# A decoder layer on one core: context clipping on GpSimd, two tiles projected chunk by chunk, quantised roots transposed by DMA

## The chip, the core and the metric

The kernel runs on one core of a Trainium2 chip. TensorE (PE) multiplies into PSUM, VectorE (DVE), ScalarE (ACT) and GpSimd (POOL) work on what it needs and leaves, and DMAs are issued from three queues: SP's, ScalarE's and GpSimd's. Every engine and every queue carries its instructions out in the order in which they are written, and waits only on semaphores. The metric is the device time of one execution in microseconds.

## What is computed

```python
# attention among the heads of one token (x: 2 x 512 x 1024; 32 heads of 32, 8 groups)
q, k, v = x @ Wq + bq, repeat(x @ Wk + bk), repeat(x @ Wv + bv)
o = softmax(q k^T / sqrt(32)) v
x = layernorm(x + o)
# quantised product with the context (2 x 1024 x 1024)
fq(y, s, z) = (clip(round(y / s + z), 0, 255) - z) * s
x = layernorm(x + matmul(fq(x), fq(ctx)))
# feed-forward: shared squared-relu part, and a routed low-rank part
h = relu(x @ up) ** 2
x = layernorm(x + layernorm(h @ down + ((x @ fc1) @ expert * sum(top2(x @ gate))) @ fc2) ...)
```

## The kernel before, in words

The program has two blocks with a barrier between them: attention_and_cross (lines 57 to 1253) and feed_forward (from line 1283). The 1024 tokens are 8 tiles of 128. Each matrix that needs more than bf16 is split in a high and a low part, and three products replace one (split_products, line 51).

**Start.** SP loads x tile 0, then the attention weights in 8 chunks of 128 rows (load_w, 0.75 MB each), then x tile 1. Each chunk passes VectorE (prepare, L886, and prepare_lo, L893), ScalarE (split_w, L603 and L604) and GpSimd (keys_values_lo, L1132). project (L341) takes 6 matmuls for each chunk, 48 for a tile. All tiles are projected into the same two PSUM banks, so tile t waits for qkv_out(t - 1).

**One tile of attention.** transpose_x (L325), xT_hi_out (ScalarE, L584) and xT_lo_out (VectorE, L968), project, qkv_out (VectorE, L964). regroup (L201) brings q, k and v from tokens on the partitions to heads, in 8 small DMAs on SP. keys_diagonal makes k_bd on GpSimd (L1178) and ScalarE (L557), values_transpose and values_diagonal make v_bd (GpSimd, L1149). Then scores (L354), softmax_max, softmax_exp and softmax_transpose, values (L371), collect, and ungroup (L206), 8 small DMAs on SP back to tokens.

**One tile of the quantised product.** residual, first_stats, inverse_deviation_x1 (GpSimd), normalise_x1, quantise_a (ScalarE, relu), magic (VectorE, clip and rounding by a large constant), quantise_b (ScalarE, into the one buffer q1). transpose_q1 (L381) turns q1 on TensorE with 8 bf16 matmuls into a PSUM bank, q1T_out (ScalarE, L564) copies it to q1T, cross (L399) multiplies, cross_out (ScalarE) evacuates, and the second layer norm follows with row_term, add_column_term and inverse_deviation_x2 on GpSimd. x2 goes to DRAM (store_x2) and comes back by load_xk.

**The context.** 16 tiles are loaded from ScalarE's queue, pass ctx_a (ScalarE, relu), ctx_magic (VectorE, L956: minimum with 255, plus the constant) and ctx_b (ScalarE, to bf16). column_sums(0) and cross(0) need the first 8 of them, column_sums(1) all 16.

**Order.** Nothing is scheduled at run time: the order of each engine is the list of calls at the end of its function (TensorE L462 to L544, ScalarE L662 to L814, VectorE L980 to L1125, GpSimd L1187 to L1253, SP L247 to L314). In the feed-forward block first_products takes the first columns, and product(2, 0) needs u_lo of column block 2, which VectorE makes in split_u (L1813) after route(0) (L1825 to L1839).

## Time and profile before

| | |
|---|---|
| median of 3 runs | 636.34 us (636.12 to 637.76) |
| the profiled execution | 638.93 us |
| its span | 637.1 us |
| TensorE busy | 595.8 us, 94% of the span |
| VectorE, ScalarE, GpSimd busy | 378.5, 299.5, 123.0 us |
| mean granted TensorE clock | 0.985 of full speed |
| attention_and_cross on TensorE | 0 to about 210 us |

The profile is of one execution. Busy time of TensorE is modelled from pipelined matmuls, so the useful reading is where it stands idle and what ended that: the chain of work that ended last runs through TensorE for 64% of the span. Of the last 2.6 us between the profiled execution and the median nothing is known from the trace.

### The profile page before, as it was taken

The page shows a single profiled execution, that of the slowest core. Times are in us where ns is not written, and L with a number is a line of the kernel's source. Part 1 is how long each engine was busy: PE and PEld are TensorE (multiplying, and loading weights), DVE is VectorE, ACT ScalarE, POOL GpSimd, SP SyncE. Part 2 cuts the span into 40 slices and gives each one's busy share as a digit, 9 for nine tenths or more (in the row PEclk, how much of TensorE's full clock was granted, in tenths as well). Part 3 has the DMA queues.
Part 4 walks back from the last instruction along what each step waited for, and adds up shares of the span by engine and source line. Part 5 has one row for each costly group of instructions (what it writes and reads, how often), then busy time and mean ns, then how long its engine had stood idle before and what let it go on. Part 6 is the DMA issues. An engine that isn't in the chain of part 4 may idle for free.

```text
span 637.1 us, 9378 instructions
## 1 busy us (share of the span) xinstructions
PE 595.8 (94%) x3718; PEld 479.8 (75%) x3728; DVE 378.5 (59%) x515; ACT 299.5 (47%) x384; POOL 123.0 (19%) x162
## 2 busy tenths in 40 slices
PE   2789999998999879999999999999999999999993
PEld 1578877675776658788888888888888888888882
DVE  4746989789854353155235331138974565749976
ACT  4545778896684433333434333004354433323824
POOL 2711245645432022232220000000000000011000
PEclk9889999998999989999999999999999999999998
DMA  9756675583663657789888683402333336079913
GB/s 332 278 141 199 177 226 128 179 280 108 194 200 133 232 192 260 272 296 343 318 315 291 219 306 118 137 1 79 120 99 100 100 99 224 8 265 323 285 57 128
DMA packets 82252, 123.61 MB, mean 194 GB/s; under 512 B 23840, under 2 KB 50720, under 8 KB 82208
## 3 DMA queue, kind: packets, MB, share of 16 engines
q1 hardware_dynamic: 74592, 94.95, 44.5%
q0 software_dynamic: 5168, 19.40, 9.4%
q10 hardware_dynamic: 2448, 8.65, 4.1%
q8 instruction: 30, 0.49, 0.3%
q14 instruction: 14, 0.11, 0.1%
HBM read 83.13 MB, written 35.65 MB: 186 GB/s over the span
## 4 chain that ended last, share of the span: by engine, by line
PE 64%; DVE 2%; ACT 0%; issue 0%; DVEq 0%; ACTq 0%
PE psum L1552 33%; PE psum L1611 30%; PE psum L1519 0%; PE psum L1527 0%; PE psum L1528 0%; PE psum L1545 0%; DVE r_tok L1834 0%; DVE ffn_lo L1959 0%; DVE ffn_lo L1948 0%; ACT hx L1714 0%; DVE u_lo L1813 0%; ACT ffn_lo L1724 0%; DVE hx L1839 0%; PE psum L1536 0%; DVE stat_n L1940 0%
## 5 line engine op out<-in xcount | busy, mean ns | idle before, releaser
L1813 DVE TENSOR_TENSOR u_lo<-u_raw,u_hi 128x1024 fp32r<-128x1024 f32 x18 | 25.5, 1420 | 85.2 <-ACT u_hi L1650 85.2
L1552 PE MATMUL psum<-x1T_hi,u_hi 128*128 128x512 f32 x160 | 62.9, 393 | 0.7 <-DVE x1T_lo L1809 0.7
L1552 PE MATMUL psum<-x1T_hi,u_lo 128*128 128x512 f32 x160 | 62.3, 389 | 0.0
L1552 PE MATMUL psum<-x1T_lo,u_hi 128*128 128x512 f32 x160 | 62.3, 389 | 0.0
L1611 PE MATMUL psum<-x2T_lo,x2T_hi 128*128 128x512 f32 x264 | 62.1, 389 | 0.0
L1552 PE MATMUL psum<-x2T_hi,u_hi 128*128 128x512 f32 x144 | 57.0, 396 | 4.6 <-DVE u_lo L1813 4.6
L1611 PEld LDWEIGHTS psum<-x2T_lo,x2T_hi 128*128 128x128 f32 x264 | 49.6, 188 | 10.3
L1552 PE MATMUL psum<-x2T_lo,u_hi 128*128 128x512 f32 x144 | 56.8, 394 | 0.0
L1552 PE MATMUL psum<-x2T_hi,u_lo 128*128 128x512 f32 x144 | 56.6, 393 | 0.0
L341 PE MATMUL psum<-w_hi,xT_hi 128*128 128x512 f32 (+1 forms) x128 | 36.1, 364 | 15.7 <-POOL w_lo L1132 8.2
L1611 PE MATMUL psum<-x1T_hi,x2T_hi 128*128 128x512 f32 x216 | 50.4, 389 | 0.0
L1611 PE MATMUL psum<-x1T_hi,x2T_lo 128*128 128x512 f32 x216 | 50.4, 389 | 0.0
L2090 POOL DMA_DIRECT2D x1T_hi<-r_scratch x4 | 2.8, 711 | 245.3 <-PE psum L1611 245.3
L1611 PEld LDWEIGHTS psum<-x1T_hi,x2T_lo 128*128 128x128 f32 x216 | 40.6, 188 | 8.4
L1611 PEld LDWEIGHTS psum<-x1T_hi,x2T_hi 128*128 128x128 f32 x216 | 40.6, 188 | 8.4
L341 PEld LDWEIGHTS psum<-w_hi,xT_hi 128*128 128x128 f32 x128 | 21.0, 200 | 20.7 <-issue 8.8
L1552 PEld LDWEIGHTS psum<-x1T_hi,u_hi 128*128 128x128 f32 x160 | 30.1, 188 | 7.4 <-issue 0.9
L1552 PEld LDWEIGHTS psum<-x2T_hi,u_hi 128*128 128x128 f32 x144 | 27.4, 190 | 10.5 <-issue 4.7
L1552 PEld LDWEIGHTS psum<-x1T_hi,u_lo 128*128 128x128 f32 x160 | 30.0, 188 | 6.3
L1552 PEld LDWEIGHTS psum<-x1T_lo,u_hi 128*128 128x128 f32 x160 | 30.0, 188 | 5.9
L341 PE MATMUL psum<-w_hi,xT_lo 128*128 128x512 f32 (+1 forms) x128 | 34.5, 352 | 0.0
L341 PE MATMUL psum<-w_lo,xT_hi 128*128 128x512 f32 (+1 forms) x128 | 34.2, 350 | 0.0
(258 smaller groups left out, 1218.3 us busy)
## 6 DMA issues: line engine op xcount, KB each, us to landing
d_raw<-in_L_ffn_down_w_dram SPq DMA_DIRECT2D x20, 512.0 KB, 7.7
t_scratch<-d_raw SPq DMA_DIRECT2D x20, 512.0 KB, 6.8
d_raw<-t_scratch SPq DMA_DIRECT2D x20, 512.0 KB, 3.8
c_sb<-in_ctx_dram ACTq DMA_DIRECT2D x16, 512.0 KB, 3.9
u_raw<-in_L_ffn_up_w_dram SPq DMA_DIRECT2D x16, 512.0 KB, 5.3
r_scratch<-f1b SPq DMA_DIRECT2D x10, 512.0 KB, 5.7
r_scratch<-f2b SPq DMA_DIRECT2D x10, 512.0 KB, 5.9
x_sb<-in_x_dram SPq DMA_DIRECT2D x8, 512.0 KB, 4.9
```

The lines of the kernel that those rows point to most:

```text
L341: mm = pe.matmul(qkv_ps[:, c0:c1], s, v, start=(k == 0 and i == 0), stop=(k == KT - 1 and i == 2))
L1552: mm = pe.matmul(acc_b[:, product_index(m, b) % 4], s, v, start=(k == 0 and i == 0), stop=(k == KT - 1 and i == 2))
L1611: mm = pe.matmul(acc_of(phase)[:, t], a, v, start=(k == 0 and i == 0), stop=(k == NP - 1 and i == 2))
L1813: dve.tensor_tensor(u_lo[:, m % 2], u_raw[:, m % 2], u_hi[:, m % 2].bitcast(F32), ALU.subtract).then_inc(S["u_lo_done"], 1)
L2090: pool.dma_start(ob[ob_slot(s)].rearrange("p s h c -> p s (h c)"), r_dram[k * P:(k + 2) * P, n].rearrange("(s p) h c -> p s (h c)", p=P)). ...
```

## The change

ctx_magic moves from VectorE to GpSimd. Tiles 0 and 1 are projected chunk by chunk in turns as the weights come (project_early), tile 1 into the banks of the quantised product (qkv_of), and x tile 1 is loaded after weight chunk 3. The first two context loads wait for the last weight chunk. Of the 8 DMAs of regroup and of ungroup GpSimd issues 4, on semaphores of their own. transpose_q1 is an SP DMA that transposes q1 straight into q1T; the TensorE transposes and q1T_out are gone. store_x2 of the last two tiles has a semaphore of its own. All five lists of calls in attention_and_cross are written in a new order, and in the feed-forward block split_u(2) stands ahead of route(0).

```diff
+        qkv_of = lambda t: xa_ps if t == 1 else qkv_ps
+        SP_OUT = 4
+        SP_BLOCKS = 4
# sync
-                for n in range(NG):
+                for n in range(SP_BLOCKS):
                     sp.dma_start(pg[:, t % 2, n], qkv_sb[rows16(n), t % 2]).then_inc(pg_in[t % 2], 16)
+            def transpose_q1(t):
+                sp.wait_ge(S["q1_done"], t + 1)
+                if t >= 2:
+                    sp.wait_ge(S["xa_ready"], t - 1)
+                sp.dma_start_transpose(q1T[:, t % 2], q1[:]).then_inc(q1T_in[t % 2], 16)
             for k in range(KT):
                 load_w(k)
-            load_x(1)
+                if k == 3:
+                    load_x(1)
# tensor
+            def project_early(t, k):
+                if k == 0:
+                    pe.wait_ge(S["xT_lo_done"], t + 1)
+                pe.wait_ge(S["wq_lo_done"], k + 1)
+                pe.wait_ge(S["wkv_lo_done"], k + 1)
+                mm = contract(t, k)
+                if k == KT - 1:
+                    mm.then_inc(S["qkv_ready"], 1)
             def cross(t):
-                pe.wait_ge(S["q1T_done"], t + 1)
+                pe.wait_ge(q1T_in[t % 2], 16 * (t // 2 + 1))
+                if t >= 1:
+                    pe.wait_ge(S["xa_evac"], t)
             transpose_x(0)
-            project(0, 0)
+            project_early(0, 0)
             transpose_x(1)
-            project(0, 1)
-            project(1, 0)
-            project(1, 1)
+            project_early(0, 1)
+            project_early(0, 2)
+            project_early(1, 0)
+            project_early(1, 1)
+            project_early(1, 2)
+            project_early(1, 3)
+            project_early(0, 3)
+            project_early(0, 4)
+            project_early(0, 5)
             transpose_x(2)
+            project_early(0, 6)
+            project_early(0, 7)
+            project_early(1, 4)
...
+            project_early(1, 7)
+            project(2, 0)
             scores(0)
-            project(2, 0)
+            project(2, 1)
             values(0)
-            project(2, 1)
+            scores(1)
             transpose_x(3)
-            scores(1)
             project(3, 0)
...
             project(7, 0)
-            transpose_q1(3)
+            values(5)
+            cross(3)
             scores(6)
             project(7, 1)
-            cross(3)
-            values(5)
             transpose_expert(0)
             transpose_expert(1)
             column_sums(1)
             values(6)
             transpose_expert(2)
             transpose_expert(3)
-            transpose_q1(4)
             scores(7)
+            transpose_x2(0)
             cross(4)
# scalar
-            def q1T_out(t):
+                if c < 2:
+                    act.wait_ge(wraw_in[KT - 1], 48)
                 act.dma_start(c_sb[:, c % 2], c_tiles[c]).then_inc(c_in[c % 2], 16)
# gpsimd
+            def regroup(t):
+                pool.wait_ge(S["qkv_evac"], t + 1)
+                if t >= 2:
+                    pool.wait_ge(S["scores_ready"], t - 1)
+                    pool.wait_ge(S["vT_done"], t - 1)
+                for n in range(SP_BLOCKS, NG):
+                    pool.dma_start(pg[:, t % 2, n], qkv_sb[rows16(n), t % 2]).then_inc(pgp_in[t % 2], 16)
+            def ctx_magic(c):
+                pool.wait_ge(S["c_relu"], c + 1)
+                pool.tensor_scalar(c_sb[:, c % 2], c_sb[:, c % 2], QMAX, MAGIC, ALU.min, ALU.add).then_inc(S["c_magic"], 1)
# feed-forward, vector
             for k in range(KT):
                 x1T_lo_out(k)
+            split_u(2)
             route(0)
-            split_u(2)
             split_u(3)
```

On TensorE at the start, behind the chunks 0 of tile 0, the rows before are these; x_sb is tile 1 of x, and everything behind it is still tile 0:

```order
L325 MATMUL psum<-ident,x_sb 128x8x4x4 [waits xT_lo_done,x_in1]
L325 MATMUL psum<-ident,x_sb 128x8x4x4 x7
L341 MATMUL psum<-w_hi,xT_hi 128x512 [waits wkv_lo_done,wq_lo_done]
L341 MATMUL psum<-w_hi,xT_hi 128x256
L341 MATMUL psum<-w_lo,xT_hi 128x512
```

And after:

```order
L349 MATMUL psum<-ident,x_sb 128x8x4x4 [waits xT_lo_done,x_in1]
L349 MATMUL psum<-ident,x_sb 128x8x4x4 x7
L358 MATMUL psum<-w_hi,xT_hi 128x512 [waits wkv_lo_done,wq_lo_done]
...
L358 MATMUL psum<-w_hi,xT_hi 128x512 [waits wkv_lo_done,wq_lo_done,xT_lo_done]
L358 MATMUL psum<-w_hi,xT_hi 128x256
L358 MATMUL psum<-w_lo,xT_hi 128x512
```

The transposes of tile 1 stand after 6 matmuls instead of 24, and the matmul that waits for xT_lo_done again is the first of tile 1, after three chunks of tile 0.

On GpSimd behind the last weight chunk, before (v_bd from ones_bf is the column of ones, k_bd from pg is keys_diagonal):

```order
L1132 TENSOR_TENSOR w_lo<-v_bd,w_hi 128x2x8x32 [waits w_hi_done,wraw_in7]
L1142 TENSOR_SCALAR v_bd<-ones_bf,maskj 128x32 [waits wkv_lo_done]
L1142 TENSOR_SCALAR v_bd<-ones_bf,maskj 128x32 x7
L1178 TENSOR_SCALAR k_bd<-pg,maskt 128x8x32 [waits pg_in0]
L1178 TENSOR_SCALAR k_bd<-pg,maskt 128x8x32
```

And after:

```order
L1140 TENSOR_TENSOR w_lo<-v_bd,w_hi 128x2x8x32 [waits w_hi_done,wraw_in7]
L1150 TENSOR_SCALAR v_bd<-ones_bf,maskj 128x32 [waits wkv_lo_done]
L1150 TENSOR_SCALAR v_bd<-ones_bf,maskj 128x32 x7
L1196 TENSOR_SCALAR c_sb<-c_sb 128x1024 [waits c_relu]
L1187 DMA pg<-qkv_sb 128x1x96 [waits qkv_evac]
L1187 DMA pg<-qkv_sb 128x1x96 x3
L1196 TENSOR_SCALAR c_sb<-c_sb 128x1024 [waits c_relu]
L1204 TENSOR_SCALAR k_bd<-pg,maskt 128x8x32 [waits pgp_in0,pg_in0]
L1204 TENSOR_SCALAR k_bd<-pg,maskt 128x8x32
```

Two clippings of the context and four DMAs now stand between the weights and the first k_bd.

On VectorE at the start of the feed-forward block, before (lg, top and r_tok are the routing, u_lo is the low part of up_w):

```order
L1809 TENSOR_TENSOR x1T_lo<-psum,x1T_hi 128x512 [waits f_x1T_hi_done] x8
L1825 COPY lg<-psum 128x32 [waits f_logits_ready]
L1827 TENSOR_TENSOR lg<-lg,psum 128x32 [waits f_lgc_done]
...
L1839 TENSOR_SCALAR hx<-ident,r_tok 128x128 x3
L1813 TENSOR_TENSOR u_lo<-u_raw,u_hi 128x1024 [waits u_hi_done] x2
```

And after:

```order
L1867 TENSOR_TENSOR x1T_lo<-psum,x1T_hi 128x512 [waits f_x1T_hi_done] x8
L1871 TENSOR_TENSOR u_lo<-u_raw,u_hi 128x1024 [waits u_hi_done]
L1883 COPY lg<-psum 128x32 [waits f_logits_ready]
L1885 TENSOR_TENSOR lg<-lg,psum 128x32 [waits f_lgc_done]
...
L1897 TENSOR_SCALAR hx<-ident,r_tok 128x128 x3
L1871 TENSOR_TENSOR u_lo<-u_raw,u_hi 128x1024 [waits u_hi_done]
```

One of the two u_lo now stands ahead of the routing.

## Rows read from the trace of the kernel before

**Rows 1.** The page, busy us of each engine, then bandwidth in 40 slices.

```profile
PE 595.8 (94%) x3718; PEld 479.8 (75%) x3728; DVE 378.5 (59%) x515; ACT 299.5 (47%) x384; POOL 123.0 (19%) x162
...
GB/s 332 278 141 199 177 226 128 179 280 108 194 200 133 232 192 260 272 296 343 318 315 291 219 306 118 137 1 79 120 99 100 100 99 224 8 265 323 285 57 128
```

**Rows 2.** The waits of TensorE: us in total, times, longest.

```profile
PE psum L341 <- POOL w_lo L1132: 8.2, 1, 8.2
...
PE psum L399 <- ACT q1T L564: 0.6, 1, 0.6
```

**Rows 3.** Timeline of TensorE, 0 to 65: start, us, instruction, idle before it.

```profile
14.42 0.98 PE L341 MATMUL psum<-w_hi,xT_hi 128*128 128x512 f32 x2 [8.24 <-POOL w_lo L1132]
...
44.13 1.95 PE L354 MATMUL psum<-k_bd,pg 32*32 32x128 f32 x64
...
51.33 0.77 PE L371 MATMUL psum<-v_bd,smT 128*32 128x36 f32 x64 [0.25 <-DVE smT L974]
...
59.71 0.62 PE L341 MATMUL psum<-w_hi,xT_hi 128*128 128x512 f32 x2 [0.49 <-DVE xT_lo L968]
...
64.47 0.77 PE L371 MATMUL psum<-v_bd,smT 128*32 128x36 f32 x64 [0.26 <-DVE smT L974]
```

**Rows 4.** Timeline of GpSimd, 25 to 50.

```profile
25.81 1.70 POOL L1132 TENSOR_TENSOR w_lo<-v_bd,w_hi 128x512 fp32r<-128x512 f32 x1 [1.08 <-ACT w_hi L604]
27.62 2.69 POOL L1142 TENSOR_SCALAR v_bd<-ones_bf,maskj 128x32 f32<-128x32 bf16 x8
41.26 0.94 POOL L1178 TENSOR_SCALAR k_bd<-pg,maskt 128x256 f32<-128x256 f32 x2 [10.94 <-DMA pg<-qkv_sb]
44.77 1.90 POOL L1149 TENSOR_SCALAR v_bd<-vT,maskj 128x256 f32<-128x256 f32 x4 [2.57 <-DVE vT L858]
```

**Rows 5.** Timeline of SP's queue: the regroup of tile 0, issue time.

```profile
31.90 6.19 SPq L201 DMA_DIRECT2D pg<-qkv_sb  x8
```

**Rows 6.** Groups by form, GpSimd: count, busy us, mean ns, idle before.

```profile
L1185 POOL TENSOR_TENSOR f2b<-f2b,col 128x1024 f32<-128x1024 f32 x8 | 20.0, 2511 | 1.0 <-ACT f2b L571 1.0
L1149 POOL TENSOR_SCALAR v_bd<-vT,maskj 128x256 f32<-128x256 f32 x32 | 17.9, 585 | 19.3 <-DVE vT L858 19.2
...
L2072 POOL DMA_DIRECT2D s_own<-x_scratch x8 | 4.3, 541 | 35.6 <-DMA x2b_scratch<-s_own 28.6 <-DMA hx<-in_L_ffn_ln_beta_dram 7.0
```

**Rows 7.** Busy us by stretch: PE, PEld, DVE, ACT, POOL, granted clock, DMA share.

```profile
30.00:135.00 105.00, 99.89 (x1242) 80.46 (x1245) 80.03 (x115) 75.36 (x85) 41.95 (x66) 0.98 0.62 179
```

**Rows 8.** Timeline of TensorE around its waits at 105 and 150.

```profile
104.89 0.62 PE L381 MATMUL psum<-ident_bf,q 128*128 128x128 bf16 x8
105.31 0.60 PE L341 MATMUL psum<-w_hi,xT_hi 128*128 128x512 f32 x2
...
149.11 0.62 PE L381 MATMUL psum<-ident_bf,q 128*128 128x128 bf16 x8 [1.84 <-ACT q L578]
150.11 3.28 PE L354 MATMUL psum<-k_bd,pg 32*32 32x128 f32 x64 [0.38 <-ACT k_bd L557]
```

**Rows 9.** The DMA view: issues, KB each, median us to landing.

```profile
pg<-qkv_sb SPq DMA_DIRECT2D x64, 48.0 KB, 2.9
...
qkv_sb<-x_scratch SPq DMA_DIRECT2D x6, 256.0 KB, 3.5
...
o_sb<-in_L_attn_bv_dram SPq DMA_DIRECT2D x1, 128.0 KB, 11.3
```

**Rows 10.** Timeline of ScalarE, VectorE and TensorE, 224 to 237.

```profile
224.50 1.05 ACT L1650 ACTIVATE u_hi<-u_raw 128x1024 fp32r<-128x1024 f32 x1
...
227.75 0.19 DVE L1825 COPY lg<-psum 128x32 f32<-128x32 f32 x1 [4.80 <-PE psum L1536]
...
230.94 2.35 DVE L1813 TENSOR_TENSOR u_lo<-u_raw,u_hi 128x1024 fp32r<-128x1024 f32 x2
...
232.30 0.62 PE L1552 MATMUL psum<-x2T_hi,u_hi 128*128 128x512 f32 x1 [4.59 <-DVE u_lo L1813]
...
236.02 0.40 PE L1552 MATMUL psum<-x2T_hi,u_hi 128*128 128x512 f32 x1
```

More of the change, by code:

```diff
@@ L326, in transpose_x, with contract @@
                 mm.then_inc(S["xT_ready"], 1)
+            def contract(t, k):
+                st = [x[:, t % 2, k] for x in (xT_hi, xT_lo)]
+                for i in range(3):
+                    for c0, c1 in ((0, BANK), (BANK, QKV)):
+                        s, v = split_products(st, [w[:, k, c0:c1] for w in (w_hi, w_lo)])[i]
+                        mm = pe.matmul(qkv_of(t)[:, c0:c1], s, v, start=(k == 0 and i == 0), stop=(k == KT - 1 and i == 2))
+                return mm
+            def project_early(t, k):
[6 more added lines that the diff above has]
+                    mm.then_inc(S["qkv_ready"], 1)
             def project(t, part):
@@ L666, in _ @@
             split_w(3)
+            xT_hi_out(1)
             split_w(4)
@@ L691, in _ @@
             ctx_a(4)
-            softmax_exp(1)
             ctx_b(4)
@@ L1204, in _ @@
             values_ones()
+            ctx_magic(0)
+            regroup(0)
+            ctx_magic(1)
             keys_diagonal(0)
+            regroup(1)
+            ctx_magic(2)
             values_diagonal(0)
             keys_diagonal(1)
+            regroup(2)
+            ctx_magic(3)
+            ungroup(0)
             values_diagonal(1)
+            ctx_magic(4)
             keys_diagonal(2)
+            ungroup(1)
+            ctx_magic(5)
+            regroup(3)
             inverse_deviation_x1(0)
+            ctx_magic(6)
             values_diagonal(2)
```

453 lines of the change are left out of this document (224 added, 229 removed).

## The prediction

> **What bounds the kernel now.** First the page: TensorE is busy for 595.8 of 637.1 us [rows 1], so a change can win only idle TensorE time, work that TensorE loses, or time at the lower clock. Then the waits of TensorE, whose largest is 8.2 us for the first weights [rows 2], and the timeline, which says where the idle time lies. There are four places. At the start TensorE waits for weights to 14.42, and tile 1 is projected wholly behind tile 0 [rows 3]. Between 30 and 135 us it is busy for 99.9 of 105 us, GpSimd for only 42.0 [rows 7]. Around 150 it waits 1.84 and 0.38 us and does the scores of tile 7 in 3.28 us instead of 1.95 [rows 3, 8]. At 227.7 it waits 4.59 us for u_lo [rows 10]. The long products behind that have no gap that this change touches, so what is won before 236 us reaches the end unchanged.
>
> **Part A, to the first projection of tile 3** (before: 59.71 [rows 3]). It is bounded by the last weight chunk. Its low part was ready at 25.81 + 1.70 = 27.5 [rows 4]. x tile 1 (0.5 MB) now goes ahead of four chunks; at the 332 GB/s of the first slice [rows 1] that is 1.6 us, so 29.1. The last chunk of tile 0 then ends at about 30.7, as before. But tile 1 has four of its chunks done and needs four more: half a projection lasts about 4.3 us (64.47 - 0.26 - 59.71 = 4.5 with its filling [rows 3]). So tile 1 ends at 35.1, and half of tile 2 at 39.4. The scores of tile 0 need k_bd: GpSimd goes from 29.1 through 2.7 us of ones [rows 4], one clipping, four DMA issues, 2.9 us to landing [rows 9] and 0.94 us of masks [rows 4]. A clipping on GpSimd is not in the trace. From below, its tensor_scalar of 256 columns takes 0.475 us (1.90 for four [rows 4]) and four times that is 1.9; with the fixed share of the short ones taken off it is 1.35. From above, the two-input form of 1024 columns takes 2.5 [rows 6]. I take 1.5, nearer the one-input row. An issue on GpSimd takes 0.54 us (of 128 rows like these [rows 6]) to SP's 0.77 (6.19 for 8 [rows 5]); I take 0.55. So 29.1 + 2.7 + 1.5 + 2.2 + 2.9 + 0.9 = 39.3, just when TensorE is free, and the scores start at 39.5 instead of 44.13. They take 1.95, the second half of tile 2 4.3, and values(0) can begin 5.3 us behind the scores, as before (44.13 + 1.95 to 51.33 [rows 3]), so at 46.7; 0.8 for it, 1.95 for scores(1), 1.0 for the transposes of tile 3 give 50.5. Here is the price of the new order: scores(1) used to cover the copies of tile 3 and left 0.49 us [rows 3]; now 0.49 + 1.95, some 2.6 us, stand open. Tile 3 starts at 53.1. **Gain 6.6 us.** The loads of the context, held back to the last weight, cost nothing as long as ctx_a(0) ends before the ones on GpSimd do.
>
> **Part B, to the scores of tile 7** (before: 59.71 to 150.11 + 3.28 = 153.4 [rows 3, 8], 93.7 us). Five of the eight root transposes go. Each holds the next matmul back by 105.31 - 104.89 = 0.42 us [rows 8], together 2.1. The waits 0.26, 0.60 (cross(2) for q1T [rows 2]), 1.84 and 0.38 go, 3.1 us, and 1.3 us of scores at the lower clock. Against it, cross(3) and values(5) now stand ahead of project(7, 1), so nothing covers what follows it. With T its end: qkv_out to T + 1.1, GpSimd issues regroup(7) until T + 3.3 and only then clips tile 15 of the context (T + 4.8), ScalarE rounds it (T + 5.9), and column_sums(1) has to wait for that while only 1.2 us of transposes lie in front of it. That is 1.1 + 3.6 = 4.7 us of new waits. **Gain 2.1 + 3.1 + 1.3 - 4.7 = 1.8 us.** For the rest of B I followed GpSimd's list against TensorE's: the nearest meetings are the masks of v for values(1), ready within 1 us of its turn, and the masks of k for tiles 0 and 7.
>
> **Part C, to the end of the block.** Three more root transposes, 3 x 0.42 = **1.3 us**. transpose_x2(0) now stands before cross(4); it needs x2 of tile 3 stored and loaded, 3.5 us for the load [rows 9], which fits behind cross(3) by a margin of about 2 us.
>
> **Part D, the feed-forward block.** u_hi of block 2 is there at 224.50 + 1.05 = 225.6, while VectorE is idle for 4.80 us to 227.75 [rows 10]. u_lo first takes half of 2.35, 1.2 us, and is done at 226.8, before TensorE wants it at 227.7. The 4.59 us go; the routing still begins on time at 227.75. With them go the nine matmuls from 232.30 to 236.02 at 0.41 us instead of 0.23 (granted clock at the 1.2 GHz level after the wait), 1.7 us. **Gain 6.3 us.** The next thing late would be u_lo of block 3, made behind the routing at about 232; it is wanted at 239.
>
> **The load of GpSimd.** Between 31 and 131 us it now also has 15 clippings and 52 DMA issues: 15 x 1.5 + 52 x 0.55 = 51 us beside its 42.0 [rows 7], 93 of 100 us. The 42.0 holds time in which it was held up: v_bd means 585 ns against 475 for the four at 44.77 [rows 4, 6]. VectorE gives up 16 clippings, which eases that. An engine at 93% that runs in order will be late now and then; each of the eight hand-overs to TensorE may lose some tenths. I put 1.5 us for it, from the margins under 1 us named in B.
>
> The Trainium skill, SBUF — State Buffer, section "Who interferes with whom", says that GpSimd and VectorE share one pair of ports as an exclusive lock, and that a DMA issued from GpSimd waits for its descriptors while VectorE runs a two-port operation. The rows agree that something holds GpSimd up (v_bd at 585 ns against 475 [rows 4, 6]), but its issues, 541 ns in the mean, were measured beside a VectorE with little to do [rows 6]. By the rows the sum stays as it stands; by the rule the 52 issues could each cost more, and the second rival below is what that would lead to.
>
> **Sum.** 6.6 + 1.8 + 1.3 + 6.3 - 1.5 = 14.5 us. The profiled execution goes from 638.93 to 624.4; the span from 637.1 to 622.6. The median of the runs lies 2.6 us under the profiled execution, and 636.34 - 14.5 gives 621.8.
>
> **Rivals.**
> *First: the transposing DMA is late.* No such DMA is in the trace. A plain one of 256 KB lands in 3.5 us, the slowest in the view in 11.3 [rows 9]. By the order of SP the margins from q1 to cross are about 6 to 8 us for tiles 1, 3 and 4, and more for the others. Under 6 us it costs nothing; at 11.3 three to four tiles lose 3 to 5 us each, some 12 us: 634. For it speaks that q1 is a single buffer, so that quantise_b of the next tile waits too; against it that only 0.62 of the DMA time is taken there [rows 7].
> VectorE: DVE Perf Modes, section "The three transpose paths", gives 1309 ns for one 128x128 bf16 transpose by DMA; eight of them in a row would be an estimate of 10.5 us, near the slow end. No run here shows it.
> *Second, slower than before: GpSimd becomes the bound.* If a clipping takes 2.5 us like the two-input form and an issue 0.77 like SP's, the sum between 31 and 131 is 42 + 37.5 + 40 = 120 us instead of 93, 20 more than there is; the sum without its own 1.5 is 16.0, so this is 636.34 - 16.0 + 20 = 640. It decides from the point where 15 clippings and 52 issues pass 58 us; the change is slower when they pass about 74. TensorE's waits on k_bd, v_bd and column_sums would show it.
> *Third: the front is worth little.* If x tile 1 ahead of the weights and the quantisation constants ahead of prepare_lo(6) push the last chunk to 33 us, A shrinks by 4: 626. That is inside the forecast's range.
> *Fourth: more is won.* If the new waits in B are covered (4.7) and the margins hold (1.5), 615.6.
>
> **Chances.** Forecast (618 to 628) 0.58; first rival 0.12; GpSimd between the forecast and the old time 0.12, slower than it 0.10; more than forecast 0.08. The range 615 to 634 leaves out the slow rival and about half of the case between. A measurement of this kernel can tell about 0.3% (1.9 us) from no change. Faster by more than that 0.86, within 0.04, slower 0.10.
>
> **What would show it.** In the profile of the changed kernel: the first weight matmul still near 14.4, tile 1 done near 35, scores(0) near 39.5; no wait of 4.59 near 213 to 220, with u_lo ahead of the routing (D right); a wait of 3 to 4 us ahead of column_sums(1) (B right); clippings on GpSimd of 1.3 to 1.9 us and issues near 0.55. Wrong would be: TensorE waiting on q1T (first rival), or on k_bd and v_bd again and again with GpSimd above 95% (second).

## The result and the profile after

The changed kernel takes 666.38 us (median of 4 runs, 665.89 to 667.56) where the kernel before, on the same chip, takes 637.05. The ratio is 1.0459, with a 95% interval of 1.0429 to 1.0489: it is slower by 29 us, where 14.5 us less was forecast. The profiled execution took 666.45 us, its span is 664.6.

The page of the changed kernel, busy us by engine, three of the lines in 40 slices, and the group of the clippings:

```profile
PE 600.7 (90%) x3664; PEld 480.5 (72%) x3664; DVE 376.1 (57%) x499; ACT 293.2 (44%) x376; POOL 215.3 (32%) x242
...
PE   2968978785499989999999999999999999999993
...
POOL 2789999999656302224221000000000000002100
PEclk9978999798599899999999999999999999999997
...
L1196 POOL TENSOR_SCALAR c_sb<-c_sb 128x1024 f32<-128x1024 f32 x16 | 60.5, 3778 | 2.3 <-ACT c_sb L627 1.1
```

GpSimd went from 123.0 to 215.3 us busy [rows 1]. In slices 4 to 10, the middle of the attention block, it is full, while TensorE is not. Its new work is 60.5 us of clippings, 3.78 us for one. The prediction had taken 1.5, with 2.5 as the upper bound.

The waits of TensorE (us in total, times, longest), without those of the first 15 us, which are as before:

```profile
PE psum L417 <- ACT q L631: 13.0, 2, 10.6
PE psum L389 <- POOL k_bd L1204: 9.5, 2, 5.6
...
PE psum L358 <- DVE xT_lo L992: 3.9, 3, 2.7
PE psum L406 <- DVE smT L998: 3.7, 2, 3.4
```

L417 is column_sums, which waits for the rounded context; L389 is scores, which waits for the masks. Both hang on GpSimd. No row names the transposing DMA. Two stretches, to the first projection of tile 3 and from there to the end of scores(7) (the columns as in [rows 7]), and 60 to 150:

```profile
0.00:60.70 60.70, 39.68 (x368) 34.00 (x368) 33.94 (x46) 29.12 (x34) 41.30 (x49) 0.94 0.72 240
60.70:184.80 124.10, 95.80 (x1153) 71.42 (x1154) 77.26 (x102) 73.56 (x85) 112.50 (x127) 0.88 0.59 162
60.00:150.00 90.00, 77.24 (x903) 58.78 (x904) 56.94 (x76) 53.82 (x60) 86.18 (x96) 0.92 0.58 152
```

GpSimd is busy for 86.2 of 90 us, 96%. The timeline of GpSimd at its first clippings, and of TensorE at the places of [rows 3] and [rows 8]:

```profile
32.89 3.65 POOL L1196 TENSOR_SCALAR c_sb<-c_sb 128x1024 f32<-128x1024 f32 x1
36.60 2.36 POOL L1187 DMA_DIRECT2D pg<-qkv_sb  x4
39.48 3.62 POOL L1196 TENSOR_SCALAR c_sb<-c_sb 128x1024 f32<-128x1024 f32 x1 [0.52 <-ACT c_sb L627]
44.48 0.94 POOL L1204 TENSOR_SCALAR k_bd<-pg,maskt 128x256 f32<-128x256 f32 x2 [1.38 <-DMA pg<-qkv_sb]
```

```profile
45.68 3.64 PE L389 MATMUL psum<-k_bd,pg 32*32 32x128 f32 x64 [5.58 <-POOL k_bd L1204]
...
60.72 0.79 PE L358 MATMUL psum<-w_hi,xT_hi 128*128 128x512 f32 x1 [2.71 <-DVE xT_lo L992]
...
154.30 2.38 PE L389 MATMUL psum<-k_bd,pg 32*32 32x128 f32 x64 [3.88 <-POOL k_bd L1204]
...
175.64 5.55 PE L417 MATMUL psum<-q,ones_bf 128*128 128x512 bf16 x16 [10.63 <-ACT q L631]
```

The masks of k for tile 0 stand behind two clippings. The first delays GpSimd's four regroup DMAs, issued from 36.60 on; behind the second GpSimd still waits 1.38 us until a regroup DMA lands. The masks come at 44.48 in place of 41.26 [rows 4], so TensorE waits 5.58 us and has lost the whole lead of the front. The two scores above also ran 3.64 and 2.38 us in place of 1.95, and column_sums(1) 5.55 in place of 3.63: behind each wait the granted clock is low. It is 0.50 of full speed, the 1.2 GHz level, from 45.7 to 49.2, and 0.64 in the mean over column_sums(1).

One part did what was forecast. VectorE and TensorE at the start of the feed-forward block:

```profile
259.29 1.23 DVE L1871 TENSOR_TENSOR u_lo<-u_raw,u_hi 128x1024 fp32r<-128x1024 f32 x1 [2.63 <-ACT u_hi L1708]
261.49 0.19 DVE L1883 COPY lg<-psum 128x32 f32<-128x32 f32 x1 [0.97 <-PE psum L1594]
```

```profile
261.38 0.50 PE L1610 MATMUL psum<-x2T_hi,u_hi 128*128 128x512 f32 x1
```

TensorE's wait of 4.59 us [rows 10] is gone. From the first transpose of that block (245.11) to the end are 419.5 us, before 425.7 (from 211.40): 6.2 us less. All of the loss, and more (33.7 us), lies ahead of this block.

### The profile page after: what moved, and what is told of

The parts are those of the page before. It is cut to its first block, busy times and chain, and to the rows that moved or that the text cites. A ratio compares the mean times of both kernels' runs of the same rounds, so it can differ in the third digit from the quotient of the medians.

```text
span 664.6 us, 9288 instructions
## 1 busy us (share of the span) xinstructions
PE 600.7 (90%) x3664; PEld 480.5 (72%) x3664; DVE 376.1 (57%) x499; ACT 293.2 (44%) x376; POOL 215.3 (32%) x242
## 3 DMA queue, kind: packets, MB, share of 16 engines
q0 software_dynamic: 7216, 21.50, 10.2%
## 4 chain that ended last, share of the span: by engine, by line
PE 61%; DVE 1%; ACT 0%; issue 0%; ACTq 0%
PE psum L1610 31%; PE psum L1669 29%; PE psum L1577 0%; PE psum L1585 0%; PE psum L1586 0%; PE psum L1603 0%; DVE ffn_lo L2017 0%; DVE ffn_lo L2006 0%; ACT hx L1772 0%; ACT ffn_lo L1782 0%; DVE stat_n L1998 0%; DVE ffn_lo L1991 0%; DVE x1T_lo L1867 0%; PE psum L1594 0%; ACT x1T_hi L1703 0%
## 5 line engine op out<-in xcount | busy, mean ns | idle before, releaser
L1871 DVE TENSOR_TENSOR u_lo<-u_raw,u_hi 128x1024 fp32r<-128x1024 f32 x18 | 22.0, 1225 | 79.4 <-ACT u_hi L1708 79.4
L1196 POOL TENSOR_SCALAR c_sb<-c_sb 128x1024 f32<-128x1024 f32 x16 | 60.5, 3778 | 2.3 <-ACT c_sb L627 1.1
L1669 PEld LDWEIGHTS psum<-x2T_lo,x2T_hi 128*128 128x128 f32 x264 | 49.5, 188 | 10.3
L358 PE MATMUL psum<-w_hi,xT_hi 128*128 128x512 f32 (+1 forms) x128 | 38.2, 382 | 12.1 <-POOL w_lo L1140 8.2
L2132 POOL TENSOR_TENSOR s_own<-s_own,hx 128x1024 f32<-128x1024 f32 x8 | 20.9, 2610 | 42.2 <-DMA s_own<-x_scratch 42.2
```

Source lines behind the costliest of these rows:

```text
L358: mm = pe.matmul(qkv_of(t)[:, c0:c1], s, v, start=(k == 0 and i == 0), stop=(k == KT - 1 and i == 2))
L1196: pool.tensor_scalar(c_sb[:, c % 2], c_sb[:, c % 2], QMAX, MAGIC, ALU.min, ALU.add).then_inc(S["c_magic"], 1)
L1669: mm = pe.matmul(acc_of(phase)[:, t], a, v, start=(k == 0 and i == 0), stop=(k == NP - 1 and i == 2))
L1871: dve.tensor_tensor(u_lo[:, m % 2], u_raw[:, m % 2], u_hi[:, m % 2].bitcast(F32), ALU.subtract).then_inc(S["u_lo_done"], 1)
L2132: pool.tensor_tensor(flat2(s3_own[:]), flat2(s3_own[:]), beta, ALU.add).then_inc(S["beta_done"], 1)
```

## The price of a clipping

The first four runs take the suspected cost away, and measure it by itself. Of the changed kernel, e1 puts the clippings back on VectorE, e2 puts all small DMAs back on SP, e3 does both; e4 is the kernel before with an added price list.

```diff
# e1: gpsimd -> vector, 16 calls placed in VectorE's list
-                pool.tensor_scalar(c_sb[:, c % 2], c_sb[:, c % 2], QMAX, MAGIC, ALU.min, ALU.add)
+                dve.tensor_scalar(c_sb[:, c % 2], c_sb[:, c % 2], QMAX, MAGIC, ALU.min, ALU.add)
# e2: and no regroup or ungroup on GpSimd
-        SP_OUT = 4
-        SP_BLOCKS = 4
+        SP_OUT = 8
+        SP_BLOCKS = 8
# e4: gpsimd, on the idle buffer s_own, twice
+                probe(flat_s, flat_s, QMAX, MAGIC, ALU.min, ALU.add)
+                probe(flat_s, flat_s, 1.0, MAGIC, ALU.mult, ALU.add)
+                probe(flat_s, flat_s, 1.0, 1.0, ALU.mult, ALU.mult)
+                probe(flat_s, flat_s, 1.0, None, ALU.mult)
+                probe(flat_s, flat_s, QMAX, None, ALU.min)
```

> The changed kernel with only the 16 clippings of the context put back on VectorE, each in a place that fits the new lists; all else (chunkwise tiles, DMA transposes, four issues of each regroup and ungroup on GpSimd, the new order, the feed-forward edit) stays. Theory (GpSimd is the bound because a clipping takes 3.78 us there): GpSimd loses 60.5 us of work, its busy time between 60 and 185 us falls from 113 of 124 us to about 60, TensorE's waits on k_bd and on the 16th context tile go, and the time is near the forecast, 618 to 630 us. Rival (the new order, the DMA transposes or the front cost the time): 645 us or more, with waits on q1T or q in place of those on k_bd. Rival (issues on GpSimd are enough to hold it up): between, about 635 to 645.

Measured: 636.2 us (10 runs), 0.9984 of before (0.996 to 1.0007). The waits on k_bd fell from 9.5 to 1.7 us. So 30 us of the loss go with the clippings, as the theory has it, but the time is 14 us over the forecast: the clipping isn't the only fault. It lies in the range of the second rival, the issues; e3 speaks against that one.

> The changed kernel with all 8 DMAs of regroup and ungroup issued by SP again; the clippings stay on GpSimd. Theory: GpSimd loses 64 issues of 0.557 us, 35.6 us, of which some 28 lie in the saturated stretch of 125 us; it stays nearly full (113 - 28 = 85 of the stretch, with in-order waits), so part of the loss goes: 640 to 652 us. If only the sum of GpSimd's work counted, 666 - 28 = 638. Rival (the clippings hold the path one by one and the issues don't matter): 660 to 668.

Measured: 651.56 us (4 runs), ratio 1.0223 (1.0194 to 1.0252), at the end of the theory's range. Taking 35.6 us of issues off GpSimd gives 15 us, taking 60.5 us of clippings off it (e1) 30: both loads count. The gain here is net of a new wait of TensorE, 7.8 us for the expert weights.

> The changed kernel with the clippings on VectorE and all issues on SP, so that GpSimd does what it did before, and only the order, the front, the DMA transposes and the feed-forward edit are new. Theory: 618 to 630 us, within 3 us of the run with the issues left on GpSimd; the difference of those two is the worth of the shared issues. Rival (the order needs GpSimd's issues to be on time, since SP takes 0.77 us for each): 4 to 8 us slower than that run.

Measured: 641.95 us (5 runs), ratio 1.0082 (1.0052 to 1.0111). That misses the theory's range, and is 5.7 us slower than e1, as the rival has it. TensorE waits 9.1 us for the expert weights here, 2.4 in e1, since their DMA stands behind the small ones in SP's queue.

> The kernel before with 18 extra GpSimd instructions in its idle stretch of the feed-forward block, before the last add_beta, on the buffer that add_beta overwrites; they change nothing that is computed. Each form stands twice: 1024 columns with minimum and add (the clipping), multiply and add, multiply and multiply, multiply alone, minimum alone; minimum and add of 512 and of 256 columns, multiply and multiply of 256; a two-input add of 1024. Theory (a two-operation tensor_scalar of 1024 f32 columns costs 3.6 us on GpSimd by itself): all three two-operation forms 3.5 to 3.8, one operation about half, 512 columns 1.8. Rival (minimum alone is dear): multiply and multiply about 1.5, minimum 3.6. Rival (the 3.6 us in the changed kernel come from contention): the clipping takes under 2 us here. The time of the kernel should stay at 637.

Measured: 636.62 us (one run). The timeline of GpSimd: the first row is the clipping in the first pass, the others are of the second pass in the order of the list (clipping, multiply and add, multiply and multiply, multiply, minimum; behind the shorter forms the two-input add):

```profile
315.11 3.66 POOL L2105 TENSOR_SCALAR s_own<-s_own 128x1024 f32<-128x1024 f32 x1 [6.92 <-DMA x2b_scratch<-s_own]
...
335.33 3.96 POOL L2105 TENSOR_SCALAR s_own<-s_own 128x1024 f32<-128x1024 f32 x1
339.37 1.05 POOL L2105 TENSOR_SCALAR s_own<-s_own 128x1024 f32<-128x1024 f32 x1
340.51 1.05 POOL L2105 TENSOR_SCALAR s_own<-s_own 128x1024 f32<-128x1024 f32 x1
341.64 2.78 POOL L2105 TENSOR_SCALAR s_own<-s_own 128x1024 f32<-128x1024 f32 x1
344.50 2.77 POOL L2105 TENSOR_SCALAR s_own<-s_own 128x1024 f32<-128x1024 f32 x1
...
352.20 2.39 POOL L2111 TENSOR_TENSOR s_own<-s_own,hx 128x1024 f32<-128x1024 f32 x1
```

Minimum and add costs 3.66 us, multiply and add or multiply and multiply of the same shape 1.05. The price hangs on the operations, not on the two operands nor on contention: neither theory had it quite so, since multiply alone costs 2.78, more than two operations of the cheap pair. The Trainium skill, GPSIMD Engine Reference, section "Engine selection", says that one-input work on GpSimd runs at roughly line rate. The rows agree for the two forms of 1.05 us, and not for the clipping nor for one operation alone.

## The same change with a cheap clipping

min(y, 255) = 255 - relu(255 - y). So ScalarE can make relu(255 - y), GpSimd multiplies by -1 and adds, and ScalarE's second pass takes the lower side with a relu. Nothing else moves. This gives the prediction its own premise.

```diff
-                act.activation(c_sb[:, c % 2], c_sb[:, c % 2], ACT.Relu, bias=qp[:, 3:4], scale=qp[:, 5:6])
+                act.activation(c_sb[:, c % 2], c_sb[:, c % 2], ACT.Relu, bias=qp[:, 13:14], scale=qp[:, 12:13])
-                pool.tensor_scalar(c_sb[:, c % 2], c_sb[:, c % 2], QMAX, MAGIC, ALU.min, ALU.add)
+                pool.tensor_scalar(c_sb[:, c % 2], c_sb[:, c % 2], -1.0, MAGIC + QMID + QMAX, ALU.mult, ALU.add)
-                act.activation(q2[:, c // CK, c % CK], c_sb[:, c % 2], ACT.Identity, bias=so["unmagic"][:])
+                act.activation(q2[:, c // CK, c % CK], c_sb[:, c % 2], ACT.Relu, bias=so["unmagic"][:])
# the constants: qp[:, 12] = -1 / scale, qp[:, 13] = 255 - zero point, qp[:, 8] = - zero point
```

> The changed kernel with the clipping written without a minimum, and nothing else moved: ScalarE makes relu(255 - y) in place of relu(y), GpSimd multiplies by -1 and adds the large constant (the form that took 1.05 us in the price list, where minimum and add took 3.66), ScalarE takes the constant off with a relu. The 16 context tiles still pass GpSimd at the same places. This gives the prediction its own premise (1.5 us assumed). Theory (the price of the one instruction was the only fault): the forecast holds, 619 to 628 us. Rival (other terms of the forecast were wrong too, as 636 us with the clippings on VectorE suggests): the front about 4 us early in place of 6.6, and the stretch to scores(7) longer than before by some us: 628 to 634. Rival (GpSimd is held up by VectorE whatever it does): clippings near 3 us again and 650 or more.

Measured: 636.51 us (10 runs), ratio 0.9977 (0.9947 to 1.0007). A clipping takes 1.16 us in the mean. The price of the one instruction is thus 666.38 - 636.51 = 29.9 us; 14.7 us between this and the forecast have other causes. It lies above the ranges of the theory and of the first rival, though both signs of that rival are in the trace: a front some 4 to 5 us early, and a longer stretch to scores(7). The profiled execution was the fastest of its ten (632.95), so the stages below show 8.6 of the 14.7.

The places where TensorE loses time in it, and what VectorE and GpSimd did ahead of the first:

```profile
109.44 0.77 PE L406 MATMUL psum<-v_bd,smT 128*32 128x36 f32 x64 [2.84 <-DVE smT L1000]
...
138.51 0.44 PE L451 MATMUL psum<-ident,wq_own 128*128 128x128 f32 x2 [1.27 <-DMA k_bd<-in_L_ffn_expert_w_dram]
...
143.58 6.04 PE L417 MATMUL psum<-q,ones_bf 128*128 128x512 bf16 x16 [3.97 <-ACT q L631]
```

```profile
102.72 4.10 DVE L981 TENSOR_SCALAR f2b<-f2b 128x1024 f32<-128x1024 f32 x1
106.75 1.27 DVE L845 BATCH_NORM_STATS2 stat<-f2b 128x6 f32<-128x512 f32 x2
108.06 0.21 DVE L848 BATCH_NORM_AGGREGATE mv<-stat 128x2 f32<-128x12 f32 x1
108.18 1.20 DVE L1000 STREAM_TRANSPOSE smT<-u_raw 128x1024 f32<-128x1024 f32 x1
```

```profile
100.62 2.19 POOL L1189 DMA_DIRECT2D pg<-qkv_sb  x4
102.81 1.09 POOL L1198 TENSOR_SCALAR c_sb<-c_sb 128x1024 f32<-128x1024 f32 x1
103.83 2.44 POOL L1213 TENSOR_TENSOR f2b<-f2b,col 128x1024 f32<-128x1024 f32 x1
```

magic(2), the same clipping on VectorE, takes 0.69 us by itself and 4.10 here. It ends 0.5 us after GpSimd has done three pieces of work in a row (106.27). The transpose of the softmax, which TensorE waits for, is queued behind it. The Trainium skill, SBUF — State Buffer, section "Who interferes with whom", says that a VectorE instruction in a two-port mode and GpSimd lock each other out of a shared pair of ports for a whole instruction. These rows agree, with VectorE as the one that stands still; the prediction had used the rule for GpSimd's DMA issues alone, and those stayed at 0.557 us. GpSimd loses time too: two masks of k at 109.29 took 2.46 us, the first two in the kernel before 0.94 [rows 4]. The sum over the block, for normalise_x1 and magic (count, busy us, mean ns), 56 to 200 us, of the kernel before, of e5 and of e3:

```profile
L828 DVE TENSOR_SCALAR f2b<-f2b,mv,rstd 128x1024 f32<-128x1024 f32 x8 | 7.2, 905 | 0.4 <-POOL rstd L1157 0.4
L952 DVE TENSOR_SCALAR f2b<-f2b 128x1024 f32<-128x1024 f32 x8 | 5.5, 692 | 1.3 <-ACT f2b L571 1.3
```

```profile
L852 DVE TENSOR_SCALAR f2b<-f2b,mv,rstd 128x1024 f32<-128x1024 f32 x8 | 11.9, 1488 | 1.8 <-POOL rstd L1167 1.8
L981 DVE TENSOR_SCALAR f2b<-f2b 128x1024 f32<-128x1024 f32 x8 | 11.9, 1482 | 0.0
```

```profile
L849 DVE TENSOR_SCALAR f2b<-f2b,mv,rstd 128x1024 f32<-128x1024 f32 x8 | 10.7, 1342 | 1.9 <-POOL rstd L1178 1.9
L977 DVE TENSOR_SCALAR f2b<-f2b 128x1024 f32<-128x1024 f32 x8 | 8.4, 1055 | 0.0
```

From the kernel before to e5 these two alone grew by 11.1 us, nearly the 12.3 us of clippings that VectorE was rid of. But the clippings are not what they grew by: in e3, where GpSimd does only what it did before, they take 19.1 us, 6.4 of the 11.1; with the shared issues (e1) 21.5; with the clippings on GpSimd as well (e5) 23.8. In the old order the clippings on GpSimd add 0.5 (e8, 13.2 against 12.7). So most of it came with the new order; what in that order does it no run shows.

> The same with all 8 DMAs of each regroup and ungroup on SP. With the clippings on VectorE this step cost 642.0 - 636.2 = 5.8 us, of which the wait for the expert weights (9.1 in place of 2.4 us) was most. Theory (SP is late with what stands behind the issues, whatever GpSimd does): again 4 to 7 us slower than with shared issues. Rival (GpSimd's issues cost GpSimd more than they give): no slower.

Measured: 642.22 us (10 runs), ratio 1.0075 (1.0046 to 1.0103): 5.7 us slower, as expected, with 6.8 us of waiting for the expert weights. In the new order the shared issues are worth their place.

## The parts one by one

```diff
# e7: the kernel before, feed-forward, vector
+            split_u(2)
             route(0)
-            split_u(2)
# e8: the kernel before, ctx_magic from vector to gpsimd in the cheap form
# e12: e7 with qkv_of, project_early and load_x(1) behind weight chunk 3, as in the change
# e11: e5 with transpose_q1 on TensorE and q1T_out on ScalarE, as before
```

> The kernel before with one line moved: split_u(2) ahead of route(0) in the feed-forward block (part D alone). Theory: the wait of 4.59 us and the slow clock behind it go, 6.3 us: 637.1 - 6.3 = 630.8 us. Rival (another wait takes its place, for u_lo of block 3 or the routing): under 3 us.

Measured: 630.87 us (4 runs), ratio 0.9897 (0.9838 to 0.9956). Part D by itself is worth what was forecast, 6.3 us at the median (2.8 to 10.3 by the interval), and this kernel beats both the one before and the changed one.

> The kernel before with the clipping in the cheap form moved to GpSimd, each right behind a step of GpSimd's old list, no other part of the change. VectorE loses 12.3 us, GpSimd gets 16 x 1.05 = 17. Theory (before, no TensorE wait in the attention block hangs on VectorE or GpSimd for more than tenths, apart from 1.84 and 0.38 us near 150): 634 to 637 us, within 1% of before, so the clipping's place is worth little by itself. Rival (VectorE at 80 of 105 us was the hidden bound): 630 or less.

Measured: 638.78 us (10 runs), ratio 1.0015 (0.9979 to 1.0051). No difference that can be told: VectorE's 12.3 us were no bound in the kernel before, so taking them off it wins nothing even where GpSimd has room.

> The cheap-clip kernel with the root transposes back on TensorE, each at the nearest place in the new order, and q1T_out back on ScalarE; the rest as in the cheap-clip kernel. Theory (a transpose by DMA takes 0.42 us off TensorE each and is never waited for): 3.4 us slower than the cheap-clip kernel, 639 to 641. Rival (the transposing DMA is late or in the way of the other small DMAs): no slower, 636 or less. Rival (ScalarE, at 0.75 to 0.9 in this stretch, can't take 8 more copies): 643 or more.

Measured: 644.73 us (6 runs), ratio 1.0127 (1.0101 to 1.0153): 8.2 us slower than e5, in the third range. In the new order the DMA transposes are worth more than TensorE's 3.4 us; TensorE waits 2.5 us for q1T and 1.4 for xa_out, and 3.8 for smT behind a VectorE that is later than in e5.

> The kernel before with two parts of the change: tiles 0 and 1 projected chunkwise with x tile 1 loaded after weight chunk 3, and split_u(2) ahead of route(0). Clippings, issues, transposes and the order behind project(3, 0) are those of before. Theory (the front gains the 4 to 5 us seen in the other runs, and nothing behind it is tight): project(3, 0) at 55 us, the end 5 us before the run with split_u(2) alone, 626. Rival (the middle is held by ScalarE and VectorE, not by TensorE, so an earlier start only lengthens waits there): 629 to 631, with TensorE's idle time between 60 and 150 up by as much as the front gained.

Measured: 629.83 us (6 runs), ratio 0.9902 (0.9868 to 0.9936). That is 1.0 us under e7, no more than can be told. In its trace scores(0) stands at 41.01 in place of 43.86, scores(7) at 148.24 in place of 150.32, the feed-forward block at 209.25 in place of 210.10: of 2.9 us of lead 0.9 arrive. TensorE has a new wait of 2.0 us for o_sb ahead of a transpose_x, and scores(7) ran 3.29 us at a granted clock of 0.56, in e7 1.95 at full speed. And the lead itself is small against the scatter of the old start: scores(0) stands at 41.76 in e4 and 41.95 in e8, which have that start too. The rival was right in the time; that ScalarE and VectorE hold the middle is its reading, not shown beyond the one wait.

## Two repairs of the new order

```diff
# e9: e5, vector: the softmax ahead of magic(2)
             residual(3)
+            softmax_transpose(4)
             magic(2)
             first_stats(3)
-            softmax_transpose(4)
# e10: e9, and tensor:
             project(7, 0)
-            values(5)
-            cross(3)
             scores(6)
             project(7, 1)
+            values(5)
+            cross(3)
```

> The cheap-clip kernel with one line of VectorE moved: softmax_transpose(4) ahead of magic(2). In the trace of the cheap-clip kernel magic(2) took 4.10 us in place of 0.69, while GpSimd issued four DMAs, clipped and added the column term, and TensorE waited 2.84 us for the smT behind it. Theory (VectorE's instructions that read and write SBUF at the fast rate stand still while GpSimd works, and this one collision is on the path): the wait goes with the slow clock behind it, 3 to 4 us less, 632.5 to 634 at the median of 636.5. Rival (the wait for smT has another cause, or magic(2) is then late for quantise_b(2) and cross(2)): within 1 us of the cheap-clip kernel.

Measured: 634.54 us (12 runs), ratio 0.9957 (0.9938 to 0.9976), 2.0 us under e5. The wait for smT fell from 3.4 to 0.5 us in total, and magic(2) took 2.59 us at its new place. A wait of 2.8 us for qkv_sb ahead of the expert transposes took the place of e5's 1.3 for their weights. The collision was on the path, but what its end is worth is barely told from nothing (633.09 to 636.57 here, 632.95 to 639.14 in e5), and it isn't 3 to 4 us.

> The same, and values(5) and cross(3) put back behind project(7, 1) as in the kernel before, with what follows them on the other engines (cross_out(3), x2_squares(3), collect(5), ungroup(5)), and the last clipping ahead of regroup(7) on GpSimd. Theory (their old place covered the load of the expert weights and the last context tile): the waits of 1.27 and 3.97 us go, and column_sums(1) takes 3.6 us in place of 6.0 at the full clock: 5 to 8 us less than the run with the one line moved, 626 to 629. Rival (cross(3) later makes x2 of tile 3 late, and transpose_x2(0) ahead of cross(4) waits for it): 2 us less or none, with a new wait near 155.

Measured: 637.04 us (12 runs), ratio 1.0007 (0.999 to 1.0025): 2.5 us slower than e9. The theory fell. The rows of TensorE in this stretch:

```profile
141.58 3.61 PE L417 MATMUL psum<-q,ones_bf 128*128 128x512 bf16 x16 [1.42 <-ACT xa_out L646]
146.95 0.76 PE L406 MATMUL psum<-v_bd,smT 128*32 128x36 f32 x64 [1.75 <-issue]
152.89 0.66 PE L451 MATMUL psum<-ident,wq_own 128*128 128x128 f32 x2 [4.59 <-DVE xT_lo L964]
```

The waits for the expert weights and the 16th tile did go, and column_sums(1) ran at the full clock, but 4.59 us for the copy of the expert transposes came in their place. On VectorE that copy (expert_lo(1)) stands behind fc2_lo_out(0) and residual(5), which wait 2.3 and 1.3 us for their own inputs. Without cross(3) and values(5) ahead of it, scores(6) also waits 2.9 us for its masks of k. The rival named another new wait than those that came.

## The parts in the old order

Was the new order at fault for the 14.7 us? e13 to e15 add to e7 the DMA transposes, then the front, then four of eight issues on GpSimd, all in the lists of the kernel before; e16 was to add the cheap clipping.

```diff
# e13: sync, in the old list
             load_residual(2)
+            transpose_q1(0)
...
             ungroup(5)
+            transpose_q1(4)
             store_x2(3)
# e13 to e15: tensor
             scores(7)
+            w2_product(0)
             cross(4)
-            w2_product(0)
# e17: e15 without the last edit
# e18: e17 with ctx_magic on gpsimd in the cheap form
```

> The kernel before with split_u(2) ahead of route(0) and the root transposes by DMA from SP, placed in SP's old list where q1 is ready; q1T_out and the eight TensorE transposes go; w2_product(0) moved ahead of cross(4), to cover the transpose of tile 4. Theory (the parts are worth the same in the old order, so the new order is at fault): about 8 us under the run with split_u(2) alone, 623 to 626. Rival (they are worth something only in the new order; here only the 0.42 us of TensorE for each count): 627 to 628. Rival (SP's queue, which issues all 16 small DMAs of a tile here, is late with them): 631 or more, with waits on q1T.

Measured: 635.51 us (12 runs), ratio 0.9991 (0.9966 to 1.0015): 4.6 us slower than e7, with 0.7 us of waiting for q1T, in the range of the second rival but not for its reason. From scores(7) to the feed-forward block the trace has 63.8 us, e7 59.8: 4.0 us go where w2_product(0) was swapped. Another 1.8 go ahead of it, with a wait of 2.6 us for smT. TensorE, then ScalarE:

```profile
154.73 0.50 PE L441 MATMUL psum<-fc_hi,xT_hi 128*128 128x512 f32 x1 [2.27 <-DVE xT_lo L921]
```

```profile
162.83 1.21 ACT L608 ACTIVATE xa_out<-psum,rowterm,quant 128x1024 f32<-128x1024 f32 x1 [11.34 <-PE psum L407]
```

The product moved ahead waits for its own operand, cross(4) comes at 159.1 in place of 152.2, and softmax_exp(7) stands behind cross_out(4) on ScalarE, which is idle for 11.3 us.

> The same and the chunkwise front. In the old order with TensorE transposes the front gave 1.0 us (629.8 against 630.9), with scores(0) 2.9 us earlier. Theory (ScalarE held the middle, and has now 8 copies less to make): 3 to 4 us under the run without the front. Rival (something else holds the middle): within 1.5 us of it.

Measured: 634.71 us (12 runs), ratio 0.9987 (0.9963 to 1.0011): the front gives 0.8 us, as in e12, no more than can be told. The rival.

> The same and four of the eight DMAs of each regroup and ungroup issued by GpSimd, at the places where qkv_out and collect are done in the old order. Only the clipping and the order are then left of the change. Theory (a regroup is issued in half the time, about 3 us earlier): 2 to 6 us under the run before it, as in the new order. Rival (GpSimd's issues hold up VectorE or the masks): no gain.

Measured: 632.32 us (12 runs), ratio 0.9952 (0.9928 to 0.9976): 2.4 us less.

> The same and the clippings on GpSimd in the cheap form: every part of the change but its order, with the price of the clipping put right. Theory (the order is at fault): 618 to 625 us, 12 us or more under the 636.5 of the same parts in the new order. Rival (the parts hinder each other, whatever the order): 630 or more. Against the run without the clippings on GpSimd it tells what their move is worth: 0 to 3 us less if VectorE was tight, more if GpSimd's work stops VectorE's.

Measured: 649.44 us (6 runs), ratio 1.0214 (1.0182 to 1.0247). But the kernel wasn't what this text says: it held the cheap clipping and the shared issues alone, on the kernel before, without the front, the DMA transposes and the early u_lo (the wait of 4.7 us for u_lo is still in its trace). Read as what it was, against e8: with the clippings on GpSimd, sharing the issues too costs 10.7 us in the old order, where it gained 2.4 with the clippings on VectorE (e15) and 5.7 in the new order (e6 to e5).

> The kernel before with the early u_lo, the front, the DMA transposes and four of eight issues on GpSimd, clippings on VectorE, and w2_product(0) behind cross(4) as in the kernel before. The same parts with w2_product(0) ahead took 632.3 us. Theory (that swap made cross(4) 6.6 us late and cost 4 to 6 us): 626 to 629, under both the kernel before and the run with the early u_lo alone (630.9). Rival (the wait for the DMA's landing takes the place of the swap's): 631 or more, with a wait on q1T ahead of cross(4).

Measured: 630.64 us (6 runs), ratio 0.9892 (0.9858 to 0.9927). Between the two ranges: the swap had cost 1.7 us at the median, not 4 to 6, and the rival came true beside it. SP's issue and TensorE's wait:

```profile
146.26 1.26 SPq L217 DMA_TRANSPOSE q1T<-q  x1
```

```profile
147.29 2.03 PE L386 MATMUL psum<-k_bd,pg 32*32 32x128 f32 x64 [2.75 <-ACT k_bd L590]
...
151.92 5.31 PE L427 MATMUL psum<-q,q1T 128*128 128x512 bf16 x16 [2.60 <-DMA q1T<-q]
```

scores(7) starts at 147.29, 3.0 us ahead of e7; 2.60 us of waiting for the transposing DMA and 1.7 of slow clock (5.31 in place of 3.63) give that back, and cross(4) starts where it did in e7 (152.21). The front, the DMA transposes and the shared issues together win nothing over the one moved line.

> The same with the clippings on GpSimd in the cheap form, so that every part of the change is there but the order of its lists. (The run e16 was to be this, but held of the change only the shared issues and the clipping in the cheap form.) Theory (the order is at fault for the 14.7 us between the forecast and the cheap-clip kernel): 618 to 625. Rival (GpSimd, with clippings and issues in one queue, delays the regroups and masks and stops VectorE, in any order; the new order is the better of the two for that load): 636 or more, up to the 649 of e16.

Measured: 640.59 us (12 runs), ratio 1.0064 (1.004 to 1.0088). The theory fell: with every part in it the old order is 4.1 us slower than the new one (e5). Here the clippings on GpSimd cost 10.0 us against e17, at 1.05 us apiece; in the new order (e5 against e1) nothing. In e18 TensorE waits 4.9 us for k_bd, and ScalarE 7.8 us for the clipped context and 10.2 for the regrouped keys. GpSimd's first clipping and the issues behind it:

```profile
36.18 1.05 POOL L1193 TENSOR_SCALAR c_sb<-c_sb 128x1024 f32<-128x1024 f32 x1 [3.46 <-ACT c_sb L622]
37.17 2.36 POOL L1184 DMA_DIRECT2D pg<-qkv_sb  x4
```

The clipping waits for ScalarE, which in this list takes xT_hi_out(2) first, and the issues of regroup(0) wait behind it: in e17 they start at 33.38. scores(0) stands at 45.04 in place of 40.47, 4.6 us of the 6.8 by which the feed-forward block comes later than in e17. Over all clippings GpSimd stands idle 14.4 us for ScalarE, in e5 1.6. 60 to 150 us of e17, then of e18:

```profile
60.00:150.00 90.00, 83.24 (x1136) 62.46 (x1134) 82.33 (x110) 71.17 (x84) 70.01 (x107) 1.00 0.68 196
```

```profile
60.00:150.00 90.00, 81.77 (x1000) 62.60 (x999) 70.46 (x87) 63.23 (x72) 76.41 (x117) 0.96 0.68 192
```

GpSimd at 85% isn't full, and VectorE at 78% is freer than in e17; the time is lost in the order in which GpSimd comes to its work. So the loss of 14.7 us isn't the new order's alone; that order makes room for a load that the parts bring, and that won nothing over e7 in any run here. What the old order would take with the first clipping behind regroup(0) wasn't run. None of these kernels beats e7 by more than can be told.

## Why the prediction was wrong, step by step

**The load of GpSimd: the step that failed.** Its term "15 x 1.5" rested on rows of the form multiply and multiply, and its upper bound on a two-input add. Both are other operations. The right factor was 3.78, outside the bounds. The prediction said how the price of an operation that the trace doesn't show is bounded by nearest rows, and took shape as what makes a row near. The issues (0.55 forecast, 0.557 measured) were right. With the price put right by e5 the loss against the forecast falls from 44.6 to 14.7 us.

**The second rival was the right mechanism.** It named the place (waits on k_bd and column_sums, and GpSimd over 95%, came; those on v_bd didn't) and the point from which it decides (58 us): 15 x 3.78 + 52 x 0.557 = 85.7. Its own sum then gives 42 + 85.7 - 100 = 27.7 us over, 636.34 - 16.0 + 27.7 = 648. Even with the right price it falls 18 us short, since the parts that it took as won (16.0) weren't: without them the sum is 664. Its chance of 0.10 was too small.

**A (6.6).** In e5 tile 3 starts at 54.74 in place of 59.71, so 5.0 us were won there: scores(0) came at 41.38 in place of 39.5, behind a k_bd 1.04 us late. That 2.6 us would stand open ahead of tile 3 was right (2.70). In the changed kernel itself it was -1.0. But 59.71 was a late start. In that execution VectorE stood idle three times for weight DMAs, and TensorE for it:

```profile
22.91 0.61 PE L341 MATMUL psum<-w_hi,xT_hi 128*128 128x512 f32 x2 [3.75 <-DVE w_lo L893]
```

Other traces with the old start have tile 3 at 59.52 (e7), but also at 57.62 (e8), 57.35 (e4) and 56.25 (e13). Against those last three the new front (55.72 in e12) is worth 0.5 to 1.9 us: the term took the luck of one execution for something that the change removes.

"What is won before 236 us reaches the end unchanged" held where all engines were early: the attention block of e4 is that of the kernel before, its scores(0) stand 2.4 us ahead of 44.13 and its feed-forward block 2.7 ahead of 211.40. For the new front it failed: in e12 0.9 of 2.9 us arrive against e7, and none against e4 (209.25 to 208.70).

**B (1.8).** In e5 98.5 us against 93.7, so -4.8. The new wait ahead of column_sums(1) was found and nearly right (4.7 forecast, 3.97 and 2.4 of slow clock measured); the prediction had put clocks into no new wait. Missed were smT at 109 (2.84), by VectorE locked out behind GpSimd, and the expert weights (1.27), whose load lost the cover of cross(3) and values(5). The prediction saw that cover go and priced only the context's part of it.

**C (1.3).** 58.4 us in e5 against 58.0: -0.4, with two waits for x2T_lo (1.7 us in all).

**D (6.3).** Right: 6.2 in the trace, 6.3 at the median of e7.

**The first rival** didn't come in the changed kernel: the transposing DMA landed in 3.1 to 5.1 us, median 3.7, and no wait names it. Where SP issues more, or in the old order, it does appear (waits of 1.6 us in e3 and 2.6 in e17, one landing of 10.5 us in e14). The Trainium skill, VectorE: DVE Perf Modes, section "The three transpose paths", led to an estimate of 10.5 us for the eight blocks; the median of 3.7 speaks against reading its figure eight times over.

**The third rival** didn't come: the last weight's low part was ready at 30.2 in the changed kernel and 29.95 in e5, against 29.1 forecast, not near 33. **The fourth** didn't either.

**What stays open.** Stages A to C of e5 miss the forecast by 8.6 us in one execution, and the median by 14.7. The other 6.1 are the distances of the two profiled executions from their medians, 2.6 above before the change and 3.6 below in e5. The 2.6 is about the late start: e4, without it, took 636.62. For the 3.6 no trace at the median exists. And which chain holds the block between 60 and 150 us in the old order isn't known: relief of TensorE (e12, e17) and of VectorE (e8) both won nothing.

## What to carry to other kernels

Before an instruction changes engines, time that form on the new engine, with the same operations: shape says little (1.05 or 3.66 us here). Ask then what stands behind it in the new queue: a clipping of 1.05 us that waits 3.5 us for its own input holds back the DMA issues behind it by 3.8 (e18). Take no gain from the start of one execution: the same start scattered by 3.5 us at scores(0). Try the parts one at a time: one moved line was worth as much as any combination tried here.
